# First half's norm factors on GpSimd, and bank parts and query parts taken earlier in two attention steps of a two-layer kernel

## The reference

```python
x = x + tanh(g_xattn[0]) * experts4(layernorm(x), token_ids, ctx)      # 4 experts, chosen by token id
x = x + tanh(g_ffn[0])   * bitnet_ffn(layernorm(x), w_gate, w_up, w_down)
x = x + tanh(g_xattn[1]) * attention(layernorm(x), ctx, Wq, Wk, Wv, Wo) # 16 heads of 128
x = x + tanh(g_ffn[1])   * moe(layernorm(x), ...)                       # 32 experts, top 8, and a shared one
```

## Time and profile before

| | |
|---|---|
| median of 3 runs | 549.73 us (549.22 to 551.35) |
| the profiled execution | 548.78 us, of which the span of the records is 547.0 us |
| granted clock of PE | 1.000 over the span |
| PE busy | 531.6 us (97%), with 3228 instructions |
| DVE, ACT, POOL busy | 385.7, 355.9 and 323.5 us |
| HBM read and written | 66.71 and 27.39 MB, 172 GB/s over the span |

### The profile page before, as it was taken

The page is one execution under the profiler, slowest core; times in us unless marked ns, Lnnn a source line. Parts: engine busy times, 40 slices in busy tenths (PEclk is TensorE's granted clock), DMA queues, the critical chain, the costliest instruction groups (busy, mean ns, idle before and its releaser), DMA issues.

```text
span 547.0 us, 9655 instructions
## 1 busy us (share of the span) xinstructions
PE 531.6 (97%) x3228; PEld 454.0 (83%) x3234; DVE 385.7 (71%) x822; ACT 355.9 (65%) x749; POOL 323.5 (59%) x324
## 2 busy tenths in 40 slices
PE   8999999999999999999999999999999999999997
PEld 6778867778788888998999999999998877778786
DVE  4867998799865676565655576656665767878873
ACT  5562146867687868676756655756757656797881
POOL 2669455998397897655645425435798447772230
PEclk9999999999999999999999999999999999999999
DMA  8920155610267777876587666534454745465851
GB/s 271 347 102 17 65 176 146 196 40 20 75 206 221 203 233 231 266 230 210 209 238 225 211 192 197 190 116 153 148 182 151 230 145 181 126 174 167 228 169 40
DMA packets 66544, 94.73 MB, mean 173 GB/s; under 512 B 6336, under 2 KB 38976, under 8 KB 66496
## 3 DMA queue, kind: packets, MB, share of 16 engines
q1 hardware_dynamic: 66496, 94.12, 54.9%
HBM read 66.71 MB, written 27.39 MB: 172 GB/s over the span
## 4 chain that ended last, share of the span: by engine, by line
PE 65%; POOL 10%; DVE 9%; issue 5%; ACT 5%; DMA 4%; SPq 1%; DVEq 0%; POOLq 0%; ACTq 0%
PE ps L1658 19%; PE ps L1659 19%; PE ps L1660 19%; PE ps L1791 4%; DMA cw_row<-cw_scratch 2%; DVE e_r L1569 1%; PE ps L1887 1%; DMA xr<-in_x 1%; POOL inner L658 1%; PE ps L1903 1%; DMA blk_raw<-in_w_tail 1%; DVE st L1140 1%; POOL inner L657 1%; POOL fly L652 1%; DMA k_hl<-k_scratch 1%
## 5 line engine op out<-in xcount | busy, mean ns | idle before, releaser
L677 POOL TENSOR_TENSOR probs<-probs,rsum 128x512 f32<-128x512 f32 x64 | 66.5, 1043 | 55.0 <-DVE rsum L1336 54.7
L1331 DVE TENSOR_REDUCE nmax<-ps 128x2 f32<-128x512 f32 x64 | 44.0, 688 | 31.3 <-PE ps L1660 30.9
L1013 ACT ACTIVATE probs<-ps,nmax 128x256 f32<-128x256 f32 x128 | 59.8, 481 | 1.7 <-DVE nmax L1331 1.6
L1098 ACT ACTIVATE e_hi<-e_r 128x512 fp32r<-128x512 f32 x64 | 40.3, 629 | 25.9 <-DVE e_r L1569 25.5
L594 POOL TENSOR_TENSOR kv_w_lo<-blk_raw,kv_w_hi 128x1024 fp32r<-128x1024 f32 x16 | 38.9, 2428 | 24.0 <-ACT kv_w_hi L846 24.0
L1322 DVE TENSOR_TENSOR pT_lo<-ps,pT_hi 128x512 fp32r<-128x512 f32 x64 | 43.8, 686 | 11.8 <-ACT pT_hi L1019 11.3
L1327 DVE TENSOR_TENSOR oT_lo<-ps,oT_hi 128x512 fp32r<-128x512 f32 x32 | 22.1, 692 | 39.7 <-ACT oT_hi L1023 39.7
L800 POOL TENSOR_TENSOR e_lo<-e_sq,e_hi 128x512 fp32r<-128x512 f32 x19 | 24.6, 1295 | 43.2 <-ACT e_sq L1104 43.0
L1019 ACT ACTIVATE pT_hi<-ps 128x512 fp32r<-128x512 f32 x64 | 38.3, 600 | 17.1 <-PE ps L1791 17.0
L1569 DVE SCALAR_TENSOR_TENSOR e_r<-ps,cw_row 128x512 f32<-128x512 f32 x64 | 43.3, 685 | 8.4 <-PE ps L1660 6.5
L600 POOL TENSOR_TENSOR k_hl<-k_hl 128x512 fp32r<-128x512 f32 x20 | 25.9, 1298 | 39.5 <-ACT k_hl L938 37.3
(11 more groups left out here) (315 smaller groups left out, 1856.7 us busy)
## 6 DMA issues: line engine op xcount, KB each, us to landing
cw_row<-cw_scratch SPq DMA_DIRECT2D x64, 256.0 KB, 3.5
v_hl<-v_scratch SPq DMA_DIRECT2D x24, 512.0 KB, 3.5
blk_raw<-in_w_blocks SPq DMA_DIRECT2D x22, 512.0 KB, 4.6
k_scratch<-kv_out SPq DMA_DIRECT2D x32, 256.0 KB, 3.7
v_scratch<-kv_out SPq DMA_DIRECT2D x32, 256.0 KB, 3.3
v_scratch<-kv_hi SPq DMA_DIRECT2D x24, 256.0 KB, 2.7
k_hl<-k_scratch SPq DMA_DIRECT2D x12, 512.0 KB, 3.4
k_hl<-k_scratch SPq DMA_DIRECT2D x20, 256.0 KB, 4.7
```

Of the source, the lines that this page charges most:

```text
L677: nc.gpsimd.tensor_tensor(probs[:, b, :, :], probs[:, b, :, :], rsum[:, b, :].unsqueeze(2).to_broadcast([P, 2, S]), ALU.mult).then_inc(pro ...
L1013: last = nc.scalar.activation(probs[:, b, t, :], ps[:, S_BANK[b], t * S:(t + 1) * S], ACT.Exp, bias=nmax[:, b, t:t + 1], accum_out=esum[:, ...
L1098: nc.scalar.activation(e_hi[i % 4][:, :], e_r[i % 2][:, :], ACT.Square).then_inc(e_hi_done, 1)
L1331: V.tensor_reduce(nmax[:, b, :], ps[:, S_BANK[b], :].rearrange("p (t k) -> p t k", t=2), AX.X, ALU.max, negate=True).then_inc(max_done, 1)
```

## The change

The three Newton rounds and the first guess of the first half's second norm move from DVE to POOL: DVE only aggregates at i = 7, waits for `ln_ready` at i = 8 and writes h. All later counts of `ln_counted` and `ln_ready` rise by one. POOL makes these factors ahead of its wait for `h_ready`; the low parts of blocks, keys and values that stood there follow as before.

In steps 1 and 11 (`OUT_BANK_FIRST`) ACT takes the bank part "m" + u and probs_high(u-1, 1) ahead of exponent(u, 0), and query_high(u+2) ahead of exponent(u, 1); DVE takes the bank part and probs_low(u-1, 1) ahead of take_max(u, 1), and query_low(u+2) ahead of both sums' inverses. In step 27 POOL's shared_low(3) moves behind normalise(27, 1).

```diff
+        OUT_BANK_FIRST = (1, 11)
...
-            pool.wait_ge(h_ready, NG + 1)
-            block_low(7)
-            pool.wait_ge(q2_clipped, NT)
-            key_low(0)
-            key_low(1)
-            value_low(0)
-            block_low(8)
-            block_low(9)
...
+            norm_factors(0, 1)
+            pool.wait_ge(h_ready, NG + 1)
+            block_low(7)
+            pool.wait_ge(q2_clipped, NT)
+            key_low(0)
+            key_low(1)
+            value_low(0)
+            block_low(8)
+            block_low(9)
...
                 normalise(u, 0)
-                if u == 27:
-                    shared_low(3)
                 if u:
                     value_low(u)
                 if u == 25:
                     shared_low(0)
                 normalise(u, 1)
+                if u == 27:
+                    shared_low(3)
...
                 for b in range(GB):
-                    if u:
+                    if u and (b == 0 or u not in OUT_BANK_FIRST):
                         probs_high(u - 1, b)
-                    if u < NU:
-                        exponent(u, b)
-                    if b == 0:
+                    if b == 0 and u in OUT_BANK_FIRST:
                         take("m" + str(u))
                         if "m" + str(u) in TASK_IN_STEP:
                             take_task(0, TASK_IN_STEP["m" + str(u)], 1)
+                        probs_high(u - 1, 1)
+                    if u < NU:
+                        exponent(u, b)
+                    if b == 0 and u in OUT_BANK_FIRST:
+                        query_high(u + 2)
...
-                if i == NT:
-                    newton(0, GN, 1)
-                elif i == NT + 1:
+                if i == NT + 1:
                     norm_lo(1, 0, pair_of["N", 0])
...
                 if i == NT - 1:
-                    factors_begin(0, GN)
+                    dve.wait_ge(dve_step, steps[0])
+                    aggregate(0)
                 elif i == NT:
-                    newton(0, GN, 2)
+                    dve.wait_ge(ln_ready, 1)
                     scaled(0).then_inc(h_ready, 1)
...
-                if u < NU:
+                if u < NU and u not in OUT_BANK_FIRST:
                     take_max(u, 1)
                 fill_low("m" + str(u))
                 step_task_low("m" + str(u))
...
                     probs_low(u - 1, 1)
+                if u in OUT_BANK_FIRST:
+                    take_max(u, 1)
+                    query_low(u + 2)
                 if u < NU:
                     invert_sum(u, 0)
-                if u + 2 < NU:
+                if u + 2 < NU and u not in OUT_BANK_FIRST:
                     query_low(u + 2)
```

More of the change, by code:

```diff
@@ L773, in _ @@
                 if u == 3:
-                    norm_factors(1, 1)
+                    norm_factors(1, 2)
                 elif u == 19:
-                    norm_factors(0, 2)
+                    norm_factors(0, 3)
                 elif u == 24:
@@ L807, in _ @@
                 if i == 3:
-                    norm_factors(1, 3)
+                    norm_factors(1, 4)
                 elif i == 12:
@@ L1072, in _ @@
                             take_task(0, TASK_IN_STEP["m" + str(u)], 1)
+                        probs_high(u - 1, 1)
[3 more added lines that the diff above has]
+                        query_high(u + 2)
+                    if b == 0:
+                        if u not in OUT_BANK_FIRST:
+                            take("m" + str(u))
+                            if "m" + str(u) in TASK_IN_STEP:
+                                take_task(0, TASK_IN_STEP["m" + str(u)], 1)
                         if u in (25, 26):
@@ L1352, in normalise @@
             def normalise(k, tiles):
-                dve.wait_ge(ln_ready, k + tiles[0] // GN)
+                dve.wait_ge(ln_ready, k + 1 + tiles[0] // GN)
                 for n in tiles:
```

## The result

The kernel with the change takes 545.92 us (median of 8 runs, 544.38 to 547.24), the kernel before 549.3 us (8 runs beside it, 547.59 to 551.35). The ratio is 0.9937 [0.9917, 0.9956], so the change is worth 3.5 us, between 2.4 and 4.6; the medians alone lie 3.4 us apart. The profiled execution took 545.86 us.

What follows compares the result with a forecast made beforehand. PE, busy 97% of the span, was taken as the bound, so only shortening its stalls helps. 0.68 + 0.75 + 0.79 + 0.5 = 2.7 us off the 549.73 us median gave 547.0 us, with an 8-in-10 range of 546.0 to 548.9.

Steps and rivals of the forecast that it cites:

- Part 1: Norm factors moved to POOL: PE's stall before h at 143.36 goes, gain 0.68 us.
- held small operations: Rival, chance 0.08: DVE's small operations between 136 and 138 are held by POOL's, price 0.45 us, total 547.5 us.
- the lock on the shared ports: Rule against part 1: DVE and GpSimd share a port pair exclusively, each DVE operation held by up to 0.23 us.
- The slower rival, late factors: Chance 0.04: POOL's 14 operations are held by DVE's work, factors come late, total 551.4 us.
- DVE's 141.34: Time DVE reaches its last two Newton rounds, kept unmoved; factors due about 139.6, some 1.7 us of room.
- Part 2: Step 1, bank part ahead of exponents and maximum: gain 0.75 us, between 0.65 and 0.84.
- The count of hand-overs: Step 1: DVE operations followed one by one, PE going on at 164.32 instead of 165.16, gain 0.84 us.
- the second stall: Step 1: PE's wait for the query's low part, ending at 165.16, 0.4 us long.
- Part 3: Step 11, transposed norm's low part taking the maximum's place: PE's 0.89 us stall shrinks, gain 0.79 us.
- Part 4: Step 27, shared low part behind the multiplication: 0.76 us stall goes, 0.25 us returns in step 28, gain 0.5 us.
- a wait comes back elsewhere: Rival, chance 0.2: one gain is met by the output copy, POOL or ACT's query copy; gain 1.6 us, total 548.1.
- within 0.5%: Chance 0.54 that the measured time is within 0.5% (2.75 us) of no change; faster 0.42, slower 0.04.

Runs made afterwards that it cites:

- again: The changed kernel run once more, unaltered, for a second trace: 545.6 us, ratio 0.9937 to the kernel before.
- before: The kernel without the change, first trace: 549.3 us (median of 8 runs), profiled execution 548.78 us.
- key_later: Changed kernel, in step 1 ACT's key and weight block copies behind probabilities and bank part, query part ahead of exponents and maximum: 546.0 us, ratio 0.9947.
- The singles: Norm factors on POOL alone, new order in steps 1 and 11 alone, step 27 move alone, each against the kernel before: 0.9978, 0.9969, 0.9991.
- again2: The changed kernel run again, unaltered, for a third trace: 546.13 us, ratio 0.9944 to the kernel before.
- store_wait: Changed kernel with SP issuing the stores of step 0's filling unit only after step 2's keys have landed: 546.96 us, ratio 0.9972.
- after: The kernel with the change, first trace: 545.92 us (median of 8 runs), ratio 0.9937, profiled execution 545.86 us.
- steps_only: The kernel before with the new order in steps 1 and 11 alone: 546.42 us, ratio 0.9969.
- null2: The kernel before, unchanged, for a third trace: 548.22 us, ratio 0.9985.
- output_early: key_later with step 0's output copied and lowered earlier in step 1, POOL's value low part behind the second multiplication: 545.7 us, ratio 0.9941.
- better: key_later with the shared expert's low part moved on from step 27 to behind both multiplications of step 28: 546.31 us, ratio 0.9945.

## Why the prediction came out as it did

**Part 1, right.** Taken at 0.68 us, measured 0.72. POOL's operations stand at 0.28 us as in the earlier trace rows; there DVE had gone idle after the sixth of them (from 438.0 us, the 2.26 us in the row's brackets), and here it works beside most of the 14, so that this trace is the better witness. The rival of held small operations didn't happen: DVE's operation at 137.03, in the midst of POOL's, took 0.21 us, and its eight instances of the loop over i took 213 to 214 ns with or without POOL beside them. The Trainium skill, "SBUF — State Buffer", section "Who interferes with whom", exempts a DVE instruction with at most one SBUF input outside its 2-port modes from the lock on the shared ports. The prediction applied the lock without this exemption. The row agrees with the exemption, if an operation on one column is outside those modes, which no run here shows. The slower rival, late factors, didn't happen either: 1.0 us of room was left, not 1.7. The prediction did not move DVE's 141.34, but the early Newton round had stood ahead of it too: DVE came to h at 140.44, 0.9 us earlier, 0.2 of which is the shorter front. The room was big enough for it not to matter.

**Part 2, right in kind, mis-sized, with a cause that wasn't seen.** The gain of the order was taken at 0.75 us of 0.65 to 0.84; it is 0.90. The count of hand-overs was right as it stood: it ended at 164.32, 0.29 us behind PE's own earliest time (162.59 + 1.44 = 164.03), and 0.29 us of the second stall is what again still has, where the query's part is just late. It was the discount from 0.84 to 0.75 that nothing bore out. What the prediction left out is that ACT stood at the landing of step 2's keys ahead of all this, a chain that isn't PE's own. That wait was in the trace of before, 0.63 us long. It moves the step by 1.0 us between traces of one kernel, and a single trace of each would have given a loss of 0.13 us (17.89 to 18.02) for an edit that gains 0.9.

**Part 3, right.** Taken at 0.79, measured 0.80 (1.12 to 0.32 us between the two passes), all in one stall.

**Part 4, right.** Taken at 0.5 after 0.25 back, measured 0.5 after 0.23 to 0.28 back, in the step and for the cause that were named.

**The rival "a wait comes back elsewhere"** didn't happen to the changed kernel: its stretch after step 1 is as long as before's (30.09 against 30.15). It did happen to key_later, at the output copy, the very place it named. So the cover was thin but there.

**The sum.** 0.72 + 0.9 + 0.80 + 0.5 = 2.9 us, against 2.7 forecast. Off 548.5 us, the median of the kernel before in the later comparisons (548.34, 548.49 and 548.75), that is 545.6 us and a ratio of 0.9947, inside all three intervals of the changed kernel. The singles say the same, with wide intervals: 0.22% + 0.31% + 0.09% = 0.62%, and 1.0 + 1.9 + 0.15 = 3.1 us by their medians. That the two first profiled executions lie 2.9 us apart as well (548.78 and 545.86) is luck: step 1 lost 0.13 us between them, and the front and the late stretch, which hold nothing of the change, gave 0.2 and 0.7 us.

**The step that failed** is the last one, from the sum to the number; the four mechanisms stand. The forecast off the median was 547.0 us, and 545.92 was measured: 1.1 us lower, and 0.08 us below the range. Three terms make it up. About 0.4 us is the anchor: 549.73 us was the median of 3 runs, the 8 runs beside the change, the same 3 among them, gave 549.3, and the 25 to 31 runs of each later comparison gave 1.0 to 1.4 us less than the anchor. About 0.2 us is the sum, nearly all of it the term of step 1, 0.75 us taken and 0.90 measured. The other 0.5 us is in no stall that the change touches, and it didn't come again as a difference of medians: 3.4 us in the first comparison, 2.9 and 2.6 in the next two (3.5, 3.5 and 3.1 by the ratios). And the range was too short at its lower end: the largest gains of the four parts are 0.68 + 0.84 + 0.79 + 0.76 = 3.1 us, which off 549.73 is 546.7, so that 0.7 us was left for the anchor and the spread together, where the median of before alone fell by up to 1.4. With 0.2 us more in the sum, 2.9 us lies above the bound of 0.5% (2.75), where 2.7 lay below it; the weight on "within 0.5%" hung on that.

**Open.** Whether the change has a part in the 0.5 us can't be told from three traces each, but the traces show where their spread sits. In the late stretch it is mostly one pass of PE, at 460.56 us in the trace of before, which stands 0.3 to 1.4 us behind the pass ahead of it in the fourteen traces. It hangs on ACT, which stands 0.8 to 1.9 us at the landing of a weight block; here ACT in again and in again2, one and the same kernel:

```profile
453.83 1.06 ACT L849 ACTIVATE ex_hi<-blk_raw 128x1024 fp32r<-128x1024 f32 x1 [0.88 <-DMA blk_raw<-in_w_tail]
```

```profile
455.08 1.06 ACT L849 ACTIVATE ex_hi<-blk_raw 128x1024 fp32r<-128x1024 f32 x1 [1.92 <-DMA blk_raw<-in_w_tail]
```

Their late stretches are 60.0 and 61.1 us. So this is a second load whose landing spreads. Two more passes, at 515.06 and 518.23 us, vary by 0.6 and 0.3 us. What decides between the two landings of the keys is not settled.

## What to carry to other kernels

In this kernel, whose PE is busy for 97%, each edit was worth the stall that it removed, less what came back behind it. Read it as the distance between starts of the same passes, stretch by stretch, and take more than one trace of each kernel, or a transfer's spread is booked on the edit. Before an order on an engine is credited or blamed, look at what that engine stood behind; a DMA landing ahead of the reordered instructions can hide the gain or double the stall. It helps to set the length of a step against the time of the landing over all traces: here the one less the other had two values, 0.90 us apart, one for each order. And when a forecast lies within a few tenths of a bound, the anchor matters as much as the sum: take it from both the median and the profiled execution, and let the range take in their difference.

## What the runs showed of the hardware

The same load of step 2's keys, by the same instruction, took from 3.5 to 4.2 us in some traces and 4.8 to 4.9 us in others, from issue to ACT's copy. Over the eleven traces in which ACT waits for it, it goes with how soon the store of step 0's values is issued behind it: 4.81, 4.82 and 4.87 us at 1.19, 1.29 and 1.21 us behind; 3.47 to 3.88 us at 1.43 to 1.50; 4.15 at 1.61; 3.69 with the store held back to 3.69. That is a correlation of one load in one place. store_wait agrees with it but doesn't decide it, since the early landing came without it as well.

The records of the load's packets show what is late. It is 128 packets of 2 KB, and in every trace 115 of them are done 2.8 to 3.2 us after the issue. The last one is done after 3.05 to 3.63 us in eleven traces, and after 4.29 to 4.41 us in after, steps_only and null2, where the last eight packets take 0.8 to 0.9 us. So the long landing is a tail of a few packets, not a slower load. The packets of the stores begin 2.5 to 2.8 us after the load's issue, in the early and in the late traces alike; in store_wait, where they begin at 4.60, the load's last packet is done at 3.18 us, no earlier than with them in output_early (3.05). The three traces in which ACT doesn't wait for this load fit the correlation: 3.61, 3.05 and 3.47 us at 1.34, 1.33 and 1.47 us behind (key_later, output_early, better).
